# Dense row streams that run through all stages of a graph network, and whole-chunk accumulation in its first mean stage

## The reference, cut to what matters

```python
x1 = x + gcn(relu(norm(x)))           # degree-weighted sum over edges, by src
x2 = x1 + sage(relu(norm(x1)))        # two layers, each a mean over edges, by dst
y  = x2 + norm(mlp update(x2))        # messages from a small network, mean by dst
out = y + relu(mean layer(y))         # mean over edges, by src
```

## Time and profile before

| what | value |
|---|---|
| time, median of 3 runs (lowest, highest) | 6238.43 us (6237.41, 6254.63) |
| span of the profiled execution (its own time is not listed apart) | 6243.6 us |
| busy share PE, DVE, ACT, POOL | 68%, 66%, 59%, 61% |
| TensorE matmuls, all instructions | 25124, 88780 |
| bytes moved, mean rate | 878.84 MB, 141 GB/s |

### The profile page before, as it was taken

The page is one execution under the profiler, slowest core; times in us unless marked ns, Lnnn a source line. Parts: engine busy times, 40 slices in busy tenths (PEclk is TensorE's granted clock), DMA queues, the critical chain, the costliest instruction groups (busy, mean ns, idle before and its releaser), DMA issues. The chain is left out here.

```text
span 6243.6 us, 88780 instructions
## 1 busy us (share of the span) xinstructions
PE 4227.3 (68%) x25124; PEld 3337.9 (53%) x25124; DVE 4147.6 (66%) x20553; ACT 3656.1 (59%) x9152; POOL 3838.7 (61%) x3228
## 2 busy tenths in 40 slices
PE   1173777777566766998958888886888846545444
PEld 1052555556455555777736666664666634434333
DVE  1094777778699995776747777785999945434334
ACT  0003767767577774776746677774877845434333
POOL 6605666675577765776747677765777654544554
PEclk7596888888788887999979999998999967667666
DMA  9903656666466664666658788884555531211221
GB/s 251 311 2 112 181 154 172 167 166 169 115 153 151 148 144 113 146 144 132 130 147 220 209 225 216 225 204 113 136 132 128 122 77 58 76 53 63 66 65 36
DMA packets 891523, 878.84 MB, mean 141 GB/s; under 512 B 131106, under 2 KB 671660, under 8 KB 890962
## 3 DMA queue, kind: packets, MB, share of 16 engines
q1 hardware_dynamic: 546568, 575.48, 29.0%
q0 software_dynamic: 224000, 235.91, 22.7%
q10 hardware_dynamic: 120460, 61.78, 3.7%
HBM read 345.70 MB, written 533.16 MB: 141 GB/s over the span
## 5 line engine op out<-in xcount | busy, mean ns | idle before, releaser
L2061 POOL DMA_INDIRECT out<-final_y,leads x200 | 202.2, 1011 | 434.8 <-DVE final_y L2188 328.8
L1151 POOL DMA_INDIRECT node<-gcn_comb,leads x200 | 325.2, 1626 | 193.0 <-ACT gcn_comb L1176 92.5
L1151 POOL DMA_INDIRECT sums<-mean_comb,leads x200 | 327.6, 1638 | 154.1 <-ACT mean_comb L1176 84.4
L1151 POOL DMA_INDIRECT node<-sage_comb,leadh x200 | 329.4, 1647 | 142.4 <-DMA node<-sage_comb,leadh 60.8
L444 PE MATMUL final_p<-wT,final_hT 128*128 128x128 f32 x800 | 223.0, 393 | 274.9 <-remote 141.4
L1151 POOL DMA_INDIRECT sums<-mlp_same,leadh x200 | 325.7, 1628 | 131.4 <-issue 54.2
L1151 POOL DMA_INDIRECT node<-sage_comb,leadd x200 | 319.5, 1597 | 140.7 <-issue 54.2
L839 PE MATMUL hist<-lo,hi 128*126 128x400 f16 x800 | 162.1, 361 | 261.4 <-issue 136.3
L444 PEld LDWEIGHTS final_p<-wT,final_hT 128*128 128x128 f32 x800 | 170.8, 264 | 305.1 <-remote 144.9
L569 POOL DMA_INDIRECT mlp_a<-node,gidx x200 | 207.2, 1036 | 197.2 <-DVE mlp_v L1778 128.6
L785 DVE TENSOR_SCALAR hi<-iota,parts 128x252 f16<-128x252 f16 x400 | 146.0, 378 | 245.7 <-remote 159.0
(11 more groups left out here) (367 smaller groups left out, 17207.2 us busy)
## 6 DMA issues: line engine op xcount, KB each, us to landing
node<-b SPq DMA_DIRECT2D x400, 256.0 KB
sums<-zero_row SPq DMA_DIRECT2D x400, 256.0 KB
node<-zero_row ACTq DMA_DIRECT2D x50, 1152.0 KB
sage_dx<-in_x SPq DMA_DIRECT2D x70, 256.0 KB
out<-sage_dy SPq DMA_DIRECT2D x70, 256.0 KB
gcn_dx<-in_x SPq DMA_DIRECT2D x66, 256.0 KB
out<-gcn_dy SPq DMA_DIRECT2D x66, 256.0 KB
x_src<-xs SPq DMA_DIRECT2D x50, 256.0 KB
```

Source lines behind the costliest of these rows:

```text
L1151: pool.indirect_dma_start(table, bass.IndirectOffsetOnAxis(ap=leads[:, i * G + c, t:t + 1], axis=0), e.comb[c][:, t, :], None, element_off ...
L2061: pool.indirect_dma_start(table, bass.IndirectOffsetOnAxis(ap=idx[:, t:t + 1], axis=0), rows[:, t, :], None, bounds_check=N - 1, oob_is_er ...
```

## The change

Three dense streams (55, 54 and 54 rounds) belong to the program, with buffers, banks and semaphores of their own, and their nodes are in the order of every stage from gcn to mean. Three more (11 rounds each) live in gcn alone. The planner ends a stage when its edge nodes are all placed and nothing of the dense streams can begin within OVERHANG of the end; where the streams stand then is passed on. Which form of the residual addition a round uses (on TensorE, or on VectorE) is fixed by the stage in which its `mix_u2` falls; the TensorE form now has a step `res` on VectorE too, which is only a semaphore increment. sage1's adds become whole. All timetables are new, and dense nodes have a period of their own.

```diff
-DENSE = {"gcn": (11,) * 6, "sage1": (10,) * 3, "sage2": (10,) * 4, "mlp": (10,) * 3, "mean": (10,) * 3}
+PARTS = (55, 54, 54)
+MORE = (11, 11, 11)
+ND = len(PARTS)
...
+OVERHANG = 3000
...
-        self.next, self.end, self.deps, self.ready = 0, [], [], None
+        self.next, self.end, self.deps, self.ready = begun, [release] * begun, [], None
...
+            if left == 0 and at > over + OVERHANG:
+                break
...
+            if line.s not in carried:
+                left, over = left - 1, max(over, free[n.eng] + (0 if n.adds is None else LANDED))
...
+    dn.begun = plan.next[G:G + ND]
...
-            + ([Node("mix_u2", TENSOR, 1490), Node("res", VECTOR, 610, after=(("store", 1, 0),), give=bank)] + ln("t_") if res == VECTOR else
-               [Node("mix_u2", TENSOR, 2440)] + ln("t_", norm_after=(("store", 1, 0),), give=bank))
+            + [Node("mix_u2", TENSOR, 2440 if res == TENSOR else 1490),
+               Node("res", VECTOR, 60 if res == TENSOR else 610, after=(("store", 1, 0),))]
...
+RES = {"gcn": TENSOR, "sage1": TENSOR, "sage2": VECTOR, "mlp": VECTOR, "mean": VECTOR}
...
+        else:
+            dve.sem_inc(done, 1)
...
-                 + edge_tail(True, SCALAR) + fill_nodes(FILL))
...
+                 + edge_tail(True, SCALAR, whole=True) + fill_nodes(FILL))
...
-                    add_pair(pool, e, plan, tb.node, k.leadh, name, i, c, W1)
+                    add_pair(pool, e, plan, tb.node, k.leadd, name, i, c, W1)
...
-                    combine_columns(nc, e.p[c], e.same[c], h[c]).then_inc(e.done[c], 1)
+                    combine_columns(nc, e.p[c], e.same[c], h[c], True).then_inc(e.done[c], 1)
...
-            for d in range(len(dn.many)):
-                dense_sync(sp, dn, inp, out, "end", dn.many[d], d)
```

More of the change, by code:

```diff
@@ L274, with __init__ @@
 class Plan:
-    def __init__(self, streams, many, period, when):
+    def __init__(self, streams, begun, many, period, when, carried):
         lines = []
@@ L293, in __init__ @@
         every = [line for own in lines for line in own]
+        left, over = sum(line.many for line in every if line.s not in carried), 0
         for line in every:
@@ L1191, in gcn_phase @@
                  + edge_tail(False, None, bank="edge") + fill_nodes(FILL))
-        for n in nodes:
-            assert n.take in (None, "edge")
-        streams = []
-        for c in L:
-            streams.append([Node(n.name, n.eng, n.length, n.after, n.main, n.take and f"edge{c % 2}", n.give and f"edge{c % 2}", n.adds)
-                            for n in nodes])
-        every = banks(8)
+        streams = [[Node(n.name, n.eng, n.length, n.after, n.main, n.take and f"edge{c % 2}", n.give and f"edge{c % 2}", n.adds)
+                    for n in nodes] for c in L]
+        every = banks(2 + len(MORE))
         e = EdgeSide(sb, sem, k, streams, every[0:2], width=WS)
-        dn = Dense(sb, sem, k, "gcn", every[2:8], False, TENSOR)
-        plan = make_plan(e.nodes + dn.nodes, "gcn")
+        more = Dense(sb, sem, "more_", MORE, every[2:], sum(PARTS))
+        plan = make_plan(e.nodes, "gcn", dn, more=more)
         x = [sb(f"x{c}", [P, T, D], F32) for c in L]
@@ L1232, in _ @@
             sp.wait_ge(e.filled, NCH * len(FILL) * 16)
-            for d in range(len(dn.many)):
-                dense_sync(sp, dn, inp, out, "end", dn.many[d], d)
+            for d in range(len(MORE)):
+                dense_sync(sp, more, inp, out, "end", MORE[d], d)
         @block.gpsimd
@@ L1382, in _ @@
                 load_xs(0, c)
-            for d in range(len(dn.many)):
-                dense_sync(sp, dn, inp, out, "first", 0, d)
             rounds(step, plan)
@@ L1979, in _ @@
                 sp.wait_ge(e.kept[c], RD * 16 + 1)
-            for d in range(len(dn.many)):
-                dense_sync(sp, dn, inp, out, "end", dn.many[d], d)
+            for d in range(ND):
+                dense_sync(sp, dn, inp, out, "end", PARTS[d], d)
         @block.gpsimd
```

228 lines of the change are left out of this document (123 added, 105 removed), and 354 rows, old and new, of the table TIMES.

## The result

The kernel after took 6308.45 us (median of 4 runs, 6278.37 to 6316.53) beside 6238.02 us before: **1.0111 times the time before, interval 1.0077 to 1.0145**. It is slower by 1.1% where 1.7% less was forecast, and 18 us above the range.

What follows compares the result with a forecast made beforehand. No single engine bounds the whole: DVE limits sage1 and mean, PE sage2 and mlp, nobody final. Terms -9 - 60 - 15 + 20 + 5 - 20 - 30 = -109; 6243.6 - 109 - 5 = 6130 us, range 5860 to 6290.

Steps and rivals of the forecast that it cites:

- What bounds the kernel, and where the ramps are: Whole kernel: no single engine bounds it; around the stage changes, 220 us of windows hold only 36 us of DVE work.
- What ends first at a stage's end: Five stage ends: add-to-gather turnarounds shrink to a floor of 10.9 us, 9 us off.
- Dense work in the ramps: Windows at the stage changes: carried dense rounds fill idle DVE time, 60 us off, at most 129.
- How the rounds spread: Dense rounds shift between stages: mean 45 us off, mlp 30 on, net 15 us off.
- Whole joins: sage1: 100 added DVE comparisons cost 20 us on, between 0 and 41.
- The empty `res` step: About 96 TensorE rounds: the added semaphore increment on DVE costs 5 us on, between 0 and 14.
- The timetables: New orders: gcn 20 us off (150 off to 100 on), final 30 off (400 off to 150 on).
- mlp's term: mlp: 7 more dense rounds cost 30 us on, between 0 and 71.
- The slower rival: final: its new order makes POOL wait more, 10 us per round or 100 us, about 6360 us; chance 0.2.
- The first rival: final keeps POOL's pace through even spacing, about 270 us more off, 5860 us; chance 0.15.
- Its opponent in the prediction: final: hand-offs out of PE stretch when POOL never pauses, speaking against the 400 us gain at POOL's pace.
- One of the prediction's own signs of being wrong: After a barrier: ACT or DVE on dense tiles wait tens of us for "remote".

Runs made afterwards that it cites:

- e15: Kernel after with halves and the old timetable in sage1 and the old timetable in mlp; 1.0083 of the kernel before, mean 759.4 us.
- e17: Kernel after with the planner constant PATIENCE at 95 ns in place of 100; 1.0310 of the kernel before.
- e8: Kernel before with whole joins in sage1 alone, its table kept; 1.0038 of the kernel before, sage1 781.2 us.
- e1: Kernel after with the old timetables in mlp and final; 1.0104 of the kernel before, mlp 1129.1 us, mean 812.9.
- e2: Kernel before with the new timetables in mlp and final, nothing carried; 1.0115 of the kernel before, mlp 1225.9 us, final 1145.2.
- e13: Kernel before with the new timetables in mlp and final, and setup's gathers paced by TensorE's counts; 1.0085 of the kernel before, mlp 1052.8 us.
- e3: Kernel after with sage1 joined in halves and sage1's old timetable; 1.0074 of the kernel before, sage1 and sage2 together 1500.7 us.
- e9: Kernel before, unchanged, run again for its profile; 0.9989 of the kernel before, mlp 990.1 us, final 793.5.
- e18: Kernel after with setup's gathers paced by TensorE's counts and mlp's first 40 gathers split; 0.9906 of the kernel before, 6190.7 us.

## Why the prediction was wrong

Step by step, against the profiled execution (6303.2 us, 59.6 above the 6243.6 of before):

- *What bounds the kernel, and where the ramps are:* right, as read.
- *What ends first at a stage's end, 9 off:* 4 off (63.5 us from last add to first gather over the five ends, now 59.5). mean's 16.6 went to 11.8 as said, the others stayed at 11.3 to 12.6 and not at the floor of 10.9.
- *Dense work in the ramps, 60 off:* DVE shows 23.5 us. The reason for halving the bound was right (ACT held to 6 us after POOL's 40th gather, again), its size was not: less than a fifth of the bound of 129 came. Without the holds it is 39.6 (condition B), which is still under 60.
- *How the rounds spread, 15 off:* the forecast counts were near in sage1 and sage2 (29 and 39, stored were 28 and 38), too low for gcn (66 against 69) and too high for mlp (37 against 34). mean gave 9 us for its three rounds fewer, not 45; e15 and e17 show that its time moves by 37 to 54 us with the same rounds, so its order is a part of the same gap as mlp's.
- *Whole joins, 20 on:* 25.7 on by itself (e8, condition B), inside the 0 to 41; in the kernel after sage1 is 30 longer, with two rounds fewer.
- *The empty `res` step, 5 on:* not measured by itself.
- *The timetables, 20 off in gcn and 30 off in final:* 7.6 and 25.9 off. final is the term that came true in A, by the table (e1, e2); in B the table gives nothing there.
- **The step that failed lies in this term: I gave the new timetables a price in gcn and final only.** mlp got 30 on for more dense rounds and nothing for its order, though the step itself says that a table fixes who goes first wherever an engine has a backlog, and mlp's PE is at 82%. The order alone costs 101 us there with the work unchanged (e2), and 63 in condition B (e13); mlp's 94.5 lie above the 71 that I took as its most. Without them the time would be 6308 - 94 = 6214 us by subtraction, a gain of 0.4%. No run reached that: e1 took mlp's loss away and gave it back in mean.

mlp is not the whole miss. The sum says 109 off, the profiled execution is 59.6 longer, 169 us apart. mlp's term is 64 of these, mean's 36, the ramps' 37, gcn's 12, sage1's 10. The ramps' DVE time shows in the stages too, so this is a list of sizes and not an exact sum. Had mlp come out at the 30 us forecast, the time of 6308 - 64 = 6244 us would have lain inside the range.

The slower rival had the mechanism (an order that waits more) and a price of the right size, 10 us a round, but I put it in final and in POOL's queue. It happened in mlp, and for the larger part not in POOL's order but in the chains through PE, ACT and DVE (69 of 96 us of waiting). The first rival, final at POOL's pace, is what condition B shows for both tables (790 to 797 us with 766 of POOL load): no table was needed for it, only hand-offs that are not held. Its opponent in the prediction, that they stretch when POOL never pauses, is what condition A does. One of the prediction's own signs of being wrong came with it: ACT on a dense tile waited 36.5 us for "remote" right after mlp's barrier.

Three things stay open: what puts a session into A or B, what releases a held hand-off, and which single steps of the new mlp order cost the time.

## What to carry to other kernels

A fixed order made from estimated lengths is worth pricing as a term of its own in every stage that it touches: here it moved single stages by 20 to 100 us with the same work, as much as or more than any structural part of the change that was measured (25.7 us for the whole join), and a table is good only together with the state in which its stage begins. Move one table at a time and read its stage, and where work can pass to the next stage, read the two together and count it (e3). Where such holds occur, keep the queue that issues indirect transfers from running unbroken beside a tight hand-over between two other engines: one wait per chunk took 127 us off setup here in condition A, and cost at most 34 us in B.

## What the runs showed of the hardware

- The same kernel on the same chip took 6247 us in one session and 5253 in another. Between the profiled executions of the kernel before and of e9 lie 985 us, and 961 of them are idle time of DVE, whose instructions took 4147.6 and 4124.3 us; PE was busy for 4227.3 and 3988.8 us, at a mean granted clock of 0.84 and 0.90.
- In condition A an engine that waits for TensorE is held while POOL issues indirect transfers back to back: about 42 us per hand-over beside 200 gathers with gaps of 0.8 us at most. The last such hold ended 26.8 us after the last gather. Where POOL paused (e18), ACT went on 2.7 us later. Pacing the gathers brought the longest hold in setup from 42 to 9.3 us. Whether the issuing or the gathers under way hold it is not shown, nor why one session has it and the other does not.
- 100 more tensor_scalar instructions on DVE left POOL's adds at 1623 ns (1654 before).
